# Second attention of a two-layer transformer kernel: the product of values and probabilities as three float32r matmuls of split operands in place of one float32 matmul

## The reference

```python
q = (hidden_states @ Wq)...   # 8 heads of width 128, rotated (cos, sin)
k = (hidden_states @ Wk)...   # 4 heads, rotated; each serves two query heads
v = (hidden_states @ Wv)...   # 4 heads
attn = softmax(causal(q k^T / sqrt(128)))
out = attn @ v                # this product is what the change rewrites
x = x + out.reshape(b, t, NH * D) @ Wo
```

## Time and profile before

| | |
|---|---|
| median of 3 runs | 1069.94 us (1066.61 to 1072.5) |
| the profiled execution | 1069.89 us, of it 1068.1 us span |
| mean granted TensorE clock | 0.946 of full speed |
| busy share of the span | PE 89%, DVE 68%, ACT 59%, POOL 31% |
| second attention | about 480 to 909 us of the span; its four heads 515 to 908 us |

### The profile page before, as it was taken

How to read it: one execution, slowest core, us unless ns; L and a number is a source line. 1 busy time by engine, 2 the same in 40 slices (tenths; PEclk the granted TensorE clock), 3 DMA queues, 4 the chain that set the end, 5 groups by cost and what they waited for, 6 DMA issues and landing times. The chain is left out here.

```text
span 1068.1 us, 16145 instructions
## 1 busy us (share of the span) xinstructions
PE 949.9 (89%) x5608; PEld 547.0 (51%) x5608; DVE 723.7 (68%) x1464; ACT 631.9 (59%) x1256; POOL 331.3 (31%) x361
## 2 busy tenths in 40 slices
PE   3699999999999978875899999999999999577998
PEld 2222222222222214324577767676767676466997
DVE  6889999999999945447445454545545454657776
ACT  3278888888888874223456555556555544334665
POOL 5700000000000000006676665848493910321222
PEclk9689999999999987997899999999999999687999
DMA  3400111110000000000000000000000000300000
GB/s 68 149 30 17 45 45 43 38 35 21 23 17 16 2 2 1 0 15 0 1 10 1 1 6 11 1 3 3 11 1 6 1 1 1 81 1 9 13 11 11
DMA packets 23369, 20.02 MB, mean 19 GB/s; under 512 B 5176, under 2 KB 17440, under 8 KB 23288
## 3 DMA queue, kind: packets, MB, share of 16 engines
q1 hardware_dynamic: 23288, 18.99, 6.0%
HBM read 14.26 MB, written 4.59 MB: 18 GB/s over the span
## 5 line engine op out<-in xcount | busy, mean ns | idle before, releaser
L674 ACT ACTIVATE probs<-score_bank 128x512 f32<-128x512 f32 x512 | 267.9, 602 | 74.3 <-PE score_bank L753 74.0
L542 DVE TENSOR_REDUCE halves<-max_bank 128x2 f32<-128x1024 f32 x256 | 298.6, 1220 | 11.1 <-PE max_bank L713 9.0
L1295 ACT ACTIVATE a_probs<-a_scores,a_lowest 128x896 f32<-128x896 f32 (+7 forms) x128 | 94.8, 741 | 112.4 <-DVE a_lowest L1290 111.8
L1540 PE MATMUL a_sum<-a_turned,a_v 128*128 128x512 f32 (+3 forms) x384 | 158.5, 500 | 0.8 <-ACT a_headsT L1469 0.6
L753 PE MATMUL score_bank<-q_stack,k_stack 50*128 50x512 bf16 x512 | 133.6, 389 | 8.1 <-ACT probs L674 6.6
L766 PE MATMUL summed<-probs,v_tile 128*32 128x512 f32 x1024 | 140.0, 620 | 0.2 <-ACT probs L674 0.2
L713 PE MATMUL max_bank<-k_stack,q_stack 48*128 48x512 bf16 x512 | 117.0, 396 | 25.1 <-DVE halves L542 25.0
L1290 DVE TENSOR_REDUCE a_lowest<-a_scores 128x1 f32<-128x896 f32 (+7 forms) x128 | 96.2, 755 | 41.1 <-PE a_scores L1284 40.6
L1531 PE MATMUL a_turn<-identity,a_probs 128*128 128x128 f32 x576 | 95.8, 276 | 4.9 <-ACT a_probs L1295 4.9
L1411 DVE COPY a_turned<-a_turn 128x512 f32<-128x512 f32 x96 | 57.5, 599 | 62.5 <-PE a_turn L1531 62.4
L469 POOL COPY v_tile<-values 128x128 f32<-128x128 f32 x16 | 4.6, 293 | 303.4 <-PE summed L766 303.3
(11 more groups left out here) (266 smaller groups left out, 1630.7 us busy)
## 6 DMA issues: line engine op xcount, KB each, us to landing
rope<-in_rope SPq DMA_DIRECT2D x8, 256.0 KB, 2.7
m_w<-in_L_ffn_mlp_w SPq DMA_DIRECT2D x8, 256.0 KB, 4.4
q_parts<-l_q_parts SPq DMA_DIRECT2D x2, 768.0 KB, 5.1
k_parts<-l_k_parts SPq DMA_DIRECT2D x2, 768.0 KB, 6.6
q_stack<-q_parts SPq DMA_DIRECT2D x30, 48.0 KB
k_stack<-k_parts SPq DMA_DIRECT2D x30, 48.0 KB
x<-in_L_attn_x SPq DMA_DIRECT2D x2, 512.0 KB, 4.2
q_stack<-shift SPq DMA_DIRECT2D x64, 2.0 KB
```

The source lines that it names most:

```text
L542: dve.reduce_max(halves[:, u % 2, half, :].rearrange("p (x t) -> p x t", x=2)[:, :, qt], max_bank[place % RING][:, :, :], AX_X).then_inc(f ...
L674: act.activation(probs[:, step % PROBS, x, :], score_bank[e % SCORES][:, :], ACT.Exp, scale=SCALE0).then_inc(prob_ready, 1)
L1295: act.activation(probs[:, k % 2, c, 0:row_width(n)], scores[n % 2][:, 0:row_width(n)], ACT.Exp, bias=lowest[:, n % 8:n % 8 + 1], accum_out ...
L1540: pe.matmul(sum_bank[:, skipped(k, j):CH], v[:, BLOCKS[k][0], j, :], turned[:, m % SLOTS, skipped(k, j):CH], start=(j == 0), stop=(TURNED_ ...
```

## The change

The value bank and the turned probabilities are each kept as two float32r parts. ACT writes every high part (now for all turns, not every second one), DVE then subtracts it from the same PSUM bank and writes the low part (likewise for all turns). A turn's bank is free, and its tile may be used, only when DVE is done. The value projections get the same pair (`raise_value`, `lower_value`). TensorE makes three float32r matmuls in place of one float32 matmul. The slots go from 4 to 3 of each part, and the whole-float copy of the input shares memory with `normed`.

```diff
-    SLOTS = 4
+    SLOTS = 3
...
+        def raise_value(act, bank, b, u, count):
+            act.wait_ge(v_ready, count)
+            act.activation(place_of(0, b, u), bank, ACT.Copy).then_inc(v_high, 1)
+
+        def lower_value(dve, bank, b, u, count):
+            dve.wait_ge(v_high, count)
+            dve.tensor_tensor(place_of(1, b, u), bank, place_of(0, b, u).bitcast(F32), ALU.subtract).then_inc(v_taken, 1)
...
-                        if what == "turn" and TURNS.index(n) % 2 == 0:
+                        if what == "turn":
                             m = TURNS.index(n)
-                            dve.wait_ge(turn_ready, from_one(g * NTURN + (m + 1)))
-                            dve.wait_ge(used, from_one(g * NTURN + max(m - SLOTS + 1, 0)))
-                            dve.tensor_copy(*copy_turned(m)).then_inc(taken[0], 1)
+                            dve.wait_ge(turned_high, from_one(g * NTURN + (m + 1)))
+                            dve.tensor_tensor(turned_of(1, m), turn_of(m), turned_of(0, m).bitcast(F32), ALU.subtract).then_inc(taken, 1)
+                        if what == "place" and n[1] >= NROT:
+                            lower_value(dve, proj_bank[:, :], *n, from_one(copies(g, *n)))
...
-                        if what == "turn" and TURNS.index(n) % 2 == 1:
+                        if what == "turn":
                             m = TURNS.index(n)
                             act.wait_ge(turn_ready, from_one(g * NTURN + (m + 1)))
                             act.wait_ge(used, from_one(g * NTURN + max(m - SLOTS + 1, 0)))
-                            act.activation(*copy_turned(m), ACT.Copy).then_inc(taken[1], 1)
+                            act.activation(turned_of(0, m), turn_of(m), ACT.Copy).then_inc(turned_high, 1)
...
-                            pe.wait_ge(taken[m % 2], from_one(g * (NTURN // 2) + m // 2))
+                            pe.wait_ge(taken, from_one(g * NTURN + max(m - 1, 0)))
...
-                            pe.wait_ge(taken[m % 2], from_one(g * (NTURN // 2) + (m // 2 + 1)))
-                            pe.matmul(sum_bank[:, skipped(k, j):CH], v[:, BLOCKS[k][0], j, :], turned[:, m % SLOTS, skipped(k, j):CH],
-                                      start=(j == 0), stop=(TURNED_BY[k] == m + 1)).then_inc(used, 1)
+                            pe.wait_ge(taken, from_one(g * NTURN + (m + 1)))
+                            left, dst = [part[:, BLOCKS[k][0], j, :] for part in v], sum_bank[:, skipped(k, j):CH]
+                            pe.matmul(dst, left[0], turned_of(0, m), start=(j == 0), stop=False)
+                            pe.matmul(dst, left[0], turned_of(1, m), start=False, stop=False)
+                            pe.matmul(dst, left[1], turned_of(0, m), start=False, stop=(TURNED_BY[k] == m + 1)).then_inc(used, 1)
```

More of the change, by code:

```diff
@@ L1166, in layer1_attention @@
         inT = [sb(f"a1_inT{i}", [P, T], F32R) for i in range(2)]
-        inT_whole = sb("a1_inT_whole", [P, T])
+        inT_whole = normed[:, :, :].rearrange("p t d -> p (t d)")
         w_whole = sb("a1_w_whole", [P, GQ + 2, D1])
@@ L1173, in layer1_attention @@
         turned_pair = sb("a1_rotated", [P, 2, CH])
-        v = sb("a1_v", [P, B, TB, D1])
+        v = [sb(f"a1_v{i}", [P, B, TB, D1], F32R) for i in range(2)]
         straight, swapped = sb("a1_straight", [P, 2, CH]), sb("a1_swapped", [P, 2, CH])
@@ L1177, in layer1_attention @@
         probs = sb("a1_probs", [P, 2, QB, S])
-        turned = sb("a1_turned", [P, SLOTS, CH])
+        turned = [sb(f"a1_turned{i}", [P, SLOTS, CH], F32R) for i in range(2)]
         headsT = sb("a1_headsT", [P, 2, CH])
@@ L1198, in layer1_attention @@
         crossed_ready, rotated = sem("crossed_ready"), sem("rotated")
-        v_ready, v_taken = sem("v_ready"), sem("v_taken")
+        v_ready, v_high, v_taken = sem("v_ready"), sem("v_high"), sem("v_taken")
         score_ready, lowest_ready, prob_ready = sem("score_ready"), sem("lowest_ready"), sem("prob_ready")
         turn_ready, used = sem("turn_ready"), sem("used")
-        taken = [sem("taken_by_vector"), sem("taken_by_scalar")]
+        turned_high, taken = sem("turned_high"), sem("turned_taken")
         heads_ready, out_ready, out_taken, added = sem("heads_ready"), sem("out_ready"), sem("out_taken"), sem("added")
@@ L1208, in from_one, with place_of @@
             return n + 1
-        def place_of(b, u):
-            return v[:, b, u % 2 * QB:(u % 2 + 1) * QB, :].rearrange("p t d -> p (t d)")
+        def place_of(i, b, u):
+            return v[i][:, b, u % 2 * QB:(u % 2 + 1) * QB, :].rearrange("p t d -> p (t d)")
+        def raise_value(act, bank, b, u, count):
[4 more added lines that the diff above has]
+            dve.tensor_tensor(place_of(1, b, u), bank, place_of(0, b, u).bitcast(F32), ALU.subtract).then_inc(v_taken, 1)
         def part_of(i, b, u):
@@ L1300, in skipped, with turned_of, turn_of @@
             return max(0, j - BLOCKS[k][2] * QB) * P
-        def copy_turned(m):
-            k, j = TURNS[m]
-            return turned[:, m % SLOTS, skipped(k, j):CH], turn_bank[m % 2][:, skipped(k, j):CH]
+        def turned_of(i, m):
+            return turned[i][:, m % SLOTS, skipped(*TURNS[m]):CH]
+        def turn_of(m):
+            return turn_bank[m % 2][:, skipped(*TURNS[m]):CH]
         def each_head(engine, body):
@@ L1387, in _ @@
                 chain = Chain(dve, dve_step)
-                for s in (straight_ready, lowest_ready, taken[0], out_taken, inverse_ready):
+                for s in (straight_ready, lowest_ready, taken, v_taken, out_taken, inverse_ready):
                     dve.sem_inc(s, 1)
@@ L1395, in _ @@
                                       ALU.subtract).then_inc(tr_low, 1)
-                for i, u in enumerate(FIRST_ROTATED):
-                    bank = first_banks[FIRST_ORDER.index(u) % 4]
+                rotated_so_far = 0
+                for at, u in enumerate(FIRST_ORDER):
+                    bank = first_banks[at % 4]
+                    if u >= NROT:
+                        lower_value(dve, bank[:, :], 0, u, from_one(u - NROT + 1))
+                        continue
+                    i, rotated_so_far = rotated_so_far, rotated_so_far + 1
                     straighten(dve, bank, u, i % 2, i + 1)
@@ L1429, in _ @@
             def _(act):
-                for s in (swapped_ready, v_taken, prob_ready, taken[1], heads_ready):
+                for s in (swapped_ready, v_high, prob_ready, turned_high, heads_ready):
                     act.sem_inc(s, 1)
@@ L1439, in _ @@
                 for i in range(2):
-                    act.wait_ge(v_ready, from_one(i + 1))
-                    act.activation(place_of(0, NROT + i), first_banks[FIRST_ORDER.index(NROT + i) % 4][:, :], ACT.Copy).then_inc(v_taken, 1)
+                    raise_value(act, first_banks[FIRST_ORDER.index(NROT + i) % 4][:, :], 0, NROT + i, from_one(i + 1))
                 for i in range(DIRECT, NROT):
@@ L1457, in body @@
                         if what == "place" and n[1] >= NROT:
-                            act.wait_ge(v_ready, from_one(copies(g, *n)))
-                            act.activation(place_of(*n), proj_bank[:, :], ACT.Copy).then_inc(v_taken, 1)
+                            raise_value(act, proj_bank[:, :], *n, from_one(copies(g, *n)))
                         if what == "score":
```

## The result

The changed kernel takes 1159.36 us (median of 4 runs, 1158.45 to 1161.35) against 1068.97 us in the same comparison: a ratio of 1.0836 (95% interval 1.081 to 1.0861), some 90 us more. The forecast was 1164.

The account below looks back on a forecast made before the run. TensorE bounded the kernel before; after the change a closed chain of ScalarE and VectorE would set the long blocks' pace. 1069.9 + 90 (seven half-heads of 12.9) + 0.5 (before the heads) + 4 (clock) = 1164 us, range 1130 to 1190.

Parts of the forecast that it names:

- the chain: Long blocks: straighten, swap, raise, subtract, lowest, exponentiate, raise, subtract, none overlapping; 12.9 us per half-head including short blocks, 90 in all.
- The round's terms: Two steps of a long block with a rotation: instruction and handoff times summing to 4.45 us, plus lowest and exponential.
- The raise-to-subtract handoff: From the end of ACT's raise to DVE's subtraction: taken as 0.04 us, from similar handoffs.
- Rival (d): Handoffs are dearer: 12 raise-to-subtract steps per half-head at 0.55 instead of 0.04, giving 1207 us; chance 0.05.
- The close: Long blocks, between second and third round: reciprocal, 0.55 wait, `a_part`, then the project; 2.4 us in all, 14 closes.
- Blocks 1 and 5: Long blocks with two rotations and two values: 19.5 us each, 3.6 more than before.
- Short blocks: Blocks without rotations, two turns against PE's two scores: +0.6 us for both, between -0.5 and +2.
- Last half-head: The half-head without projections: rounds of 4.1 to 4.9 us against PE's 3.6; nothing taken, -2 to +2.
- The clock: PE's pause before the project behind a close halves its clock: 0.7 us at a third of 14 closes; +4 taken.
- Rival (c): The clock falls for much of the long blocks, PE's work coming late into the chain: 28 us more, 1190; chance 0.15.
- What PE saves: Float32r products at 192 uses: 0.155 us per 512-column use, about 17 us in all if PE stays the bound.
- rival (a): PE stays the bound, the chain doesn't close: 1069.9 - 17 = 1053 us; chance 0.04 for faster.

Follow-up runs that it names:

- open_chain: Changed kernel's instructions, only VectorE's order changed: lowest search, rotation's cosine product (or value's low part) and close precede each turn's held subtraction; 1077.61 us.
- chain_alone: Changed kernel with its copies, subtractions and waits, but one float32 product in place of the three; 1155.26 us, ratio 1.0809.
- after_light_pool: Changed kernel with one GpSimd operation per rotation, the product with the sine table, left out; 1160.13 us, ratio 1.0828.
- low_first: Changed kernel's instructions, only VectorE's order changed: at steps with a score, the search for the lowest precedes the turn's subtraction; 1100.17 us, ratio 1.0282.
- straight_first: Changed kernel's instructions, only VectorE's order changed: a rotation's cosine product (or a value's low part) precedes the odd step's subtraction; 1136.0 us, ratio 1.0612.
- straight_close_first: As straight_first, and the close too stands ahead of the held subtraction of its step on VectorE; 1111.34 us, ratio 1.0392.
- vector_even: Changed kernel, but VectorE makes both parts of even turns itself and ScalarE the high part of odd turns only; 1127.24 us, ratio 1.0536.
- products_alone: Changed kernel's three products, but turned tiles copied once as float32r, alternately by VectorE and ScalarE; high part reused for the low; 1066.55 us.
- open_light_pool: As open_chain, but subtraction ahead of the searches again in short blocks, and GpSimd's product with the sine table left out; 1069.1 us, ratio 0.9988.
- products_light_pool: products_alone with GpSimd's product with the sine table left out of each rotation; 1056.08 us, ratio 0.9854.

## Why the prediction was right, point by point

**The mechanism** is shown. Order alone takes 82 of 90 us away (open_chain); the chain alone brings 84 of them (chain_alone); GpSimd and the products are not part of it (after_light_pool, chain_alone). Four partial openings of the chain each give back more than half of what their terms say: 59 of 63 us (low_first), 23 of 37 (straight_first), 25 of 34 (straight_close_first) and 32 of 53 (vector_even).

**The number** was helped by luck. Over the seven half-heads with projections the forecast had 90 us; the traces give 87.7, and 3.8 of these are the slower clock, which had its own term. So the blocks' own share is 84 where 90 was forecast, and this difference of 6 is what two larger errors of opposite sign leave, about 15 us too much for the closes and 8 too little for block 0.

**The round's terms** were right to a few hundredths: 6.28 measured for the second and third rounds where the sum had 6.33, and 5.56 for the fourth (660.56 to 666.12) where it had 5.64. The raise-to-subtract handoff, which had no row, was 0.04 as taken. Rival (d) is out.

**The close was mis-sized and mis-counted**, the largest error. In its rounds the wait from reciprocal to `a_part` is 0.03, not 0.55:

```profile
715.07 0.17 DVE L1435 RECIPROCAL a_inverse<-a_weight 128x4 f32<-128x4 f32 x1
715.27 0.69 DVE L1439 TENSOR_TENSOR a_part<-a_proj,a_inverse 128x512 f32<-128x512 f32 x1
717.65 0.69 DVE L1259 TENSOR_TENSOR a_straight<-a_proj,rope 128x512 f32<-128x512 f32 x1 [1.69 <-PE a_proj L1243]
```

The 0.55 idle in the earlier trace rows was something else, which I took for a price of the handoff. `a_part` also waits for the output's matmuls, and the trace of before has these just ahead of it, from 665.14 to 666.19; `a_part` starts at 666.29:

```profile
665.14 1.05 PE L1547 MATMUL a_proj<-a_wo,a_headsT 128*128 128x128 f32 x8
```

So it was a wait for TensorE; at other closes of that kernel it lasts from 0.55 to 2.54 us. And block 0 has no close (the head before ends with its own), so 10 closes have a rotation behind them and not 14. Together 4 x 2.4 + 10 x 0.5 = about 15 us too much.

**The blocks of before were cut wrongly**, in the other direction. The four windows of the earlier trace rows end at 717.05, but the next head's first transposes come at 719.34: block 7 takes 11.84. And block 0 takes 16.0, where I had set block 4's 18.13 against it. My "before" for block 0 was 2.1 us too long, its loss by as much too small in each of four heads, which makes up 8 of the 15 us. That the two partly cancel is luck.

**Blocks 1 and 5** were forecast at 19.5 and measured at 20.5 to 21.1; but part of that is where the boundary lies (the last rotation of the block ahead, 1.95 us, falls into them by first transposes), and the 21.1 hold a slow stretch of the clock (below). Blocks 4 and 5 together: 46.3 forecast, 46.1 measured, of which 0.6 is again the clock, while the forecast has 0.9 too much for their two closes.

**Short blocks**: +0.2 and +0.5 in blocks 2 and 3, 0.2 and 0.9 in 6 and 7, against +0.6 for each pair. **Last half-head**: +1.9 (34.6 to 36.5 up to its last block), against nothing taken, within its bounds.

**The clock**: granted 0.92 and 0.95 in the head's halves where it had 1.00. The size of the term, 4 us, was about right, but only a small part came the way that was forecast. That way was TensorE's pause ahead of the project behind a close, and that project at 1.2 GHz. It was seen once (lengths 0.75 and 0.63, where 0.48 and 0.39 stand in the earlier trace rows):

```profile
716.02 0.75 PE L1241 MATMUL a_proj<-a_inT,a_w_part 128*128 128x512 f32 x1 [2.94 <-DVE a_part L1439]
716.56 0.63 PE L1242 MATMUL a_proj<-a_inT,a_w_part 128*128 128x512 f32 x1
716.99 0.63 PE L1243 MATMUL a_proj<-a_inT,a_w_part 128*128 128x512 f32 x1
```

From the end of `a_part` to the straighten it cost 1.69 us instead of 1.05, 0.6 us, at 1 of 10 closes and not at a third of 14. The rest came later in the chain. Three times, in a block 1 or 5, the clock fell right behind that project; the first of these stretches is

```profile
678.60:682.00 3.40, 3.40 (x14) 2.69 (x13) 1.51 (x3) 1.79 (x3) 1.95 (x3) 0.50 0.00 0
```

and the value projection that followed was late for ScalarE:

```profile
683.75 0.60 ACT L1216 ACTIVATE a_v<-a_proj 128x512 fp32r<-128x512 f32 x1 [0.46 <-PE a_proj L1247]
```

Each of these blocks took 21.1 us instead of 20.5. And between the third and the fourth head a stretch at 0.50 (893.60 to 897.00) cost 0.6 us in block 7 and 0.8 in block 0. Together that is 0.6 + 3 x 0.57 + 1.4 = some 3.8 us. Rival (c) did not come: other slow stretches in the long blocks, such as 664.90 to 671.70, cost the chain next to nothing.

**What PE saves** was worth nothing to the forecast's sum, but rival (a) set it at 17 us. The runs give 4, or 8 with GpSimd lighter. The pitches, from one matmul's start to the next, fit in block 4 (0.81 saved, 0.84 forecast), less in block 0 (0.63); whether the saving reaches the end needed a look at GpSimd, which I had dismissed by its 64.75 of 100.50 us. Blocks 1 and 5 have two rotations close behind the four of the block ahead, and through these GpSimd works without a pause. So even had the chain been open, the time would not have been 1053. PE's busy time of a head was forecast at 80 to 85 us and is 104.99. Busy time goes by the lengths shown, which exceed the pitch (0.39 against 0.235 in the earlier trace rows) where a matmul stands alone, and I had given it by pitch; the slower clock adds to it too.

The estimate from the Trainium skill's page "TensorE: Matmul & The Clock Gate" ("Back-to-back issue gap") had the wide uses save 20.6 us; no run here comes near, the most being 8. That section gives its 216 ns as the gap of an isolated matmul and puts a stream of weight loads and matmuls at about 131 ns for 512 columns. The float32r matmuls here, which are such a stream, took 235 ns each at 2.4 GHz, so the trace is near the first of the two figures.

The short blocks should have saved 0.2 us each by the same rows (0.155 + 0.11 + 0.07 - 0.12), and gained nothing in products_alone. In blocks 2 and 6 the trace says where that went: ahead of the third score TensorE's weight load now waits for ScalarE's exponential, which it did not before.

```profile
653.43 0.19 PEld L1288 LDWEIGHTS a_scores<-a_kT,a_qT 128*128 128x128 f32 x1 [0.28 <-ACT a_probs L1303]
```

So there, too, the next resource's pace took the saving. No run with this wait removed was made, and for blocks 3 and 7 the question is open. Open is also the whole of what keeps open_light_pool 13 us above products_light_pool. Part of it are its short blocks (7.0, 9.92 and 12.7 to 13.35 where products_light_pool has 6.6, 9.46 and 11.93), part block 0 (16.0 to 17.3 against 15.4).

## What to carry to other kernels

Before giving work to engines that are half idle, write down both engines' queues for one round and follow each wait: when every instruction needs the one before it, on its own engine or on the other, the round costs the sum and not the larger load, however idle both look. Here a few rows of handoffs and durations priced a round to within 0.1 us, and the loss of all blocks to within a tenth once errors of opposite sign are set off; count how often each term occurs, block by block. If the chain closes, hold back in the queue what nobody needs at once: here the subtraction behind the next independent work, for 82 us. And a saving on the bounding engine counts only up to the next resource's pace in each block, not on average.

## What the hardware showed unexpectedly

Two dependent instructions on VectorE with a semaphore between them start 0.03 us after the first one's end (715.07 + 0.17 to 715.27), as short as a handoff between VectorE and ScalarE (0.04). In the changed kernel TensorE paused ten times ahead of a project behind a close, three times for 2.9 us (block 4) and seven times for 2.0. Once, behind a pause of 2.94 us, the project itself ran at 1.2 GHz. The nine others ran it at 2.4 GHz, and behind four of these the granted clock fell just after the project (at 678.6, 842.4, 866.3 and 931.1 us of the span). The same place of the program, behind pauses of the same length, so met either level.
